# Gate logits turned by VectorE from four copies of the gate's columns, with routed loads and orders of VectorE rearranged

## What is computed

```
xn = layernorm(x)
x  = x + attn0(xn) + ffn0(xn)          # chunked linear attention; 16 experts of 128, all applied, weighted by sigmoids
xn = layernorm(x)
x  = x + attn1(xn) + ffn1(xn)

attn1: gate_logits = xn @ gate_W                    # (T, 4); top 2, softmax -> comb
       g, v, d = xn @ Wg[m] + bg[m], ...            # m = 0..3
       h_t = a_t * h_(t-1) + sigmoid(g)*tanh(v),  a = 0.001 + 0.998*sigmoid(d)
       out = sum over m of comb[:, m] * h[m]
ffn1:  gate_logits = xn @ gate_w.T + gate_b + expert_bias   # (T, 8)
       e = argmax(gate_logits)                      # one expert per token
       out = relu(xn @ w1[e] + b1[e]) @ w2[e] + b2[e]       # 256 -> 1024 -> 256
```

## Time and profile before

| | |
|---|---|
| median of 3 timed runs | 1025.59 us (1025.57, 1025.59, 1028.11) |
| profiled execution, its own time | 1028.48 us |
| span of its profile | 1026.8 us |
| TensorE busy | 1016.7 us, 99% |
| VectorE, ScalarE, GpSimd busy | 793.2 us (77%), 626.2 us (61%), 373.9 us (36%) |
| HBM read and written | 109.20 MB, 42.27 MB |

### The profile page before, as it was taken

The page is one execution under the profiler, slowest core; times in us unless marked ns, Lnnn a source line. Parts: engine busy times, 40 slices in busy tenths (PEclk is TensorE's granted clock), DMA queues, the critical chain, the costliest instruction groups (busy, mean ns, idle before and its releaser), DMA issues.

```text
span 1026.8 us, 20067 instructions
## 1 busy us (share of the span) xinstructions
PE 1016.7 (99%) x6432; PEld 908.7 (88%) x6432; DVE 793.2 (77%) x1307; ACT 626.2 (61%) x1179; POOL 373.9 (36%) x376
## 2 busy tenths in 40 slices
PE   8999999999999999999999999999999999999998
PEld 7988989989898988989877888999999999888887
DVE  6876767667685777969789998977788778588887
ACT  4554445535444454555566667888889888566665
POOL 3443443444444453443552775122122110482000
PEclk9999999999999999999999999999999999999999
DMA  6226313122132221442546376688897885652203
GB/s 190 69 83 221 103 41 82 55 79 70 41 82 82 81 82 62 144 165 63 194 157 245 116 286 221 199 249 250 267 286 249 284 262 182 230 178 68 92 11 102
DMA packets 112130, 152.12 MB, mean 148 GB/s; under 512 B 40720, under 2 KB 80656, under 8 KB 111056
## 3 DMA queue, kind: packets, MB, share of 16 engines
q1 hardware_dynamic: 100368, 132.35, 39.3%
q0 software_dynamic: 6016, 13.51, 4.5%
q10 hardware_dynamic: 5696, 5.64, 1.7%
HBM read 109.20 MB, written 42.27 MB: 148 GB/s over the span
## 4 chain that ended last, share of the span: by engine, by line
PE 86%; DVE 4%; DMA 3%; issue 3%; SPq 2%; ACT 2%; DVEq 0%; POOL 0%; ACTq 0%; POOLq 0%
PE ps L395 17%; PE ps L393 17%; PE ps L394 17%; PE ps L1194 6%; PE ps L1195 6%; PE ps L1196 6%; DMA raw<-w 2%; PE ps L1597 2%; PE ps L1598 2%; PE ps L1599 2%; PE ps L1212 2%; PE ps L1213 2%; PE ps L1214 2%; PE ps L1263 1%; PE ps L1256 1%
## 5 line engine op out<-in xcount | busy, mean ns | idle before, releaser
L827 POOL TENSOR_TENSOR acc<-acc,ytmp 128x512 f32<-128x512 f32 x120 | 157.7, 1314 | 243.3 <-ACT ytmp L918 223.4
L1637 ACT ACTIVATE act_o<-ps,scan_bias 128x512 f32<-128x512 f32 x189 | 129.5, 688 | 98.1 <-PE ps L395 94.1
L918 ACT ACTIVATE ytmp<-ps,sel 128x256 f32<-128x256 f32 x256 | 107.3, 471 | 95.7 <-PE ps L1196 95.1
L995 DVE SCALAR_TENSOR_TENSOR hT_l<-ps,hT_h 128x512 fp32r<-128x512 f32 (+1 forms) x136 | 88.4, 655 | 87.7 <-ACT hT_h L878 87.6
L1194 PE MATMUL ps<-vals_h,hT_h 128*128 128x256 f32 x512 | 144.9, 283 | 0.1
L1195 PE MATMUL ps<-vals_l,hT_h 128*128 128x256 f32 x512 | 143.8, 281 | 0.0
L1196 PE MATMUL ps<-vals_h,hT_l 128*128 128x256 f32 x512 | 143.5, 280 | 0.0
L878 ACT ACTIVATE hT_h<-ps 128x512 fp32r<-128x512 f32 x128 | 76.3, 596 | 89.4 <-PE ps L395 84.9
L1811 POOL DMA_DIRECT2D rows<-xs_d x92 | 52.8, 575 | 175.2 <-DVE sT L2045 163.8
L1980 DVE TENSOR_TENSOR_SCAN h_b<-a_b,hstate,xs_b 128x512 f32<-128x512 f32 x63 | 88.1, 1398 | 28.2 <-ACT a_b L1644 24.8
L1040 DVE SCALAR_TENSOR_TENSOR acc<-ps,sel,acc 128x256 f32<-128x256 f32 x240 | 104.0, 475 | 3.0 <-PE ps L1196 2.9
(11 more groups left out here) (261 smaller groups left out, 2769.6 us busy)
## 6 DMA issues: line engine op xcount, KB each, us to landing
raw<-w SPq DMA_DIRECT2D x78, 512.0 KB, 5.4
x1T<-xT_d SPq DMA_DIRECT2D x16, 512.0 KB, 5.5
comb_b<-comb_d SPq DMA_DIRECT2D x8, 1024.0 KB, 8.5
xn_d<-xn SPq DMA_DIRECT2D x15, 512.0 KB, 2.9
w_small<-w SPq DMA_DIRECT2D x14, 512.0 KB, 5.1
xs_d<-zeros ACTq DMA_DIRECT2D x1, 4992.0 KB, 19.5
x_d<-x SPq DMA_DIRECT2D x8, 512.0 KB, 4.5
xT_d<-nT_h SPq DMA_DIRECT2D x8, 512.0 KB, 2.7
```

Of the source, the lines that this page charges most:

```text
L827: pool.tensor_tensor(dst[:, 2:4, :], acc[:, 2:4, :], ytmp[:, k % 2, :, :], ALU.add).then_inc(acc23, 1)
L918: act.activation(ytmp[:, k % 2, j - 2, :], yb(k, j), ACT.Copy, scale=sel[:, j, k:k + 1]).then_inc(y_23, 1)
L1637: act.activation(act_o[:, i % 2, w, :], ps[:, 3 * (i % 2) + w, :], func, bias=scan_bias[:, w, i:i + 1]).then_inc(act_g, 1)
```

## The change

The gate's weight tile `gw` gets four copies of 32 columns (12 high, 12 low, 8 of zeros), so that its product has the same 32 rows on each quarter of the partitions. ScalarE copies, of each quarter, the tokens that belong there: four copies of 32 x 128 for one of 24 x 512. VectorE transposes the 32 x 32 blocks of the result in one instruction of 128 x 128 and sums high and low parts from SBUF. `post_rows` and its four transposes on TensorE are gone, with their use of bank 6, so the bank is freed by ScalarE's last copy.

In the routed stage VectorE's `rows_out` of a small slot moves behind the first `low_e` of the next slot, and in a small slot `w2_half(n, 1)` moves behind the first `low_e`. On SP the load of b2 of a small slot is issued ahead of w2's second half, and `w1_small` is loaded in slot 1 of a round, behind b1, for slot 0. The ranking moves from slots 21 and 22 to slots 1 and 2 of round 0.

```diff
@@ -89,8 +89,6 @@
     ebias = keep("ebias", [P, E1], F32)
     gate_b = keep("gate_b", [P, E1], F32)
     logits = keep("logits", [P, TILES, NL], F32)
-    gw = keep("gw", [P, DC, 2, NL], F32R)
-    gw_raw = keep("gw_raw", [P, DC, NL], F32)
     hstate = keep("hstate", [P, MC], F32)
     neg_half = keep("neg_half", [P, JT], F32)
     pos_i = keep("pos_i", [P, TILES], I32)
@@ -156,7 +154,10 @@
     stats1 = ra("stats1", [P, JT, 6], F32)
     mv1 = ra("mv1", [P, JT, 2], F32)
     rstd1 = ra("rstd1", [P, JT], F32)
-    lgT = ra("lgT", [P, GT], F32)
+    lgT = ra("lgT", [P, JT, Q32], F32)
+    lg_rows = ra("lg_rows", [P, JT, Q32], F32)
+    gw = ra("gw", [P, DC, P // Q32, Q32], F32R)
+    gw_raw = ra("gw_raw", [P, DC, Q32], F32)
     nq = x1[:].rearrange("p j (h k) -> p (j h) k", k=DC * Q32)
     end_a = ra.at
 
@@ -362,24 +364,24 @@
     O_STEP = 11
 
 
-    USES = ["v01", "v23", "q", "g", "s", "o", "op", "lg", "lt"]
-    POST = ("t1", "lg", "lt")
+    USES = ["v01", "v23", "q", "g", "s", "o", "op", "lg"]
+    POST = ("t1", "lg")
 
     def use(g, name, first=False):
 
-        start = 2 if first else 9 * g
+        start = 2 if first else 8 * g + 1
         return start + USES.index(name)
 
     def freed(g, name, first=False):
 
-        start = 2 if first else 8 * g
+        start = 2 if first else 7 * g + 1
         return start + [u for u in USES if u != "op"].index(name) + 1
 
     def post_use(g, name):
 
         if isinstance(g, int) and g == GROUPS - 1:
             n = POST.index(name)
-            return 9 * GROUPS + n, 2, 8 * GROUPS + n + 1
+            return 8 * GROUPS + 1 + n, 2, 7 * GROUPS + n + 2
         return use(g + 1, name), None, freed(g + 1, name)
 
     def wait_alone(eng, s, value):
@@ -408,10 +410,15 @@
         act.wait_ge(side_full, n + 1)
         act.activation(dst, src, ACT.Copy).then_inc(side_hi, 1)
 
-    def logits_T(act, n):
-
-        act.wait_ge(side_full, n + 1)
-        act.activation(lgT[0:2 * NL, :], ps[0:2 * NL, 6, :], ACT.Copy).then_inc(side_free, 1)
+    def logits_T(act, g):
+
+
+        act.wait_ge(side_full, post_use(g, "lg")[0] + 1)
+        act.wait_ge(lg_turned, g + 1)
+        for q in range(P // Q32):
+            quarter = slice(q * Q32, (q + 1) * Q32)
+            tokens = ps[quarter, 6, :].rearrange("p (j t) -> p j t", j=JT)[:, :, quarter]
+            act.activation(lgT[quarter], tokens, ACT.Copy).then_inc(side_free if q == P // Q32 - 1 else lg_T, 1)
 
     def ln_stats(dve, x, st, bn, tiles=range(JT)):
         for j in tiles:
@@ -445,9 +452,12 @@
         ln_norm(dve, xn1, x1, mv1, rstd1, rs1, xn1s, g, tiles)
 
     def gate_logits(dve, g):
-        dve.wait_ge(side_full, post_use(g, "lt")[0] + 1)
-        parts = ps[:, 6, 0:JT * 2 * NL].rearrange("p (j h n) -> p j n h", j=JT, h=2)
-        dve.tensor_reduce(logits[:, bass.ds(g * JT, JT), :], parts, AX.X, ALU.add).then_inc(side_free, 1)
+        dve.wait_ge(lg_T, (P // Q32 - 1) * (g + 1))
+        dve.wait_ge(side_free, post_use(g, "lg")[2])
+        dve.transpose(lg_rows[:].rearrange("p j n -> p (j n)"), lgT[:].rearrange("p j t -> p (j t)")).then_inc(lg_turned, 1)
+        dve.wait_ge(lg_turned, g + 2)
+        parts = lg_rows[:, :, 0:2 * NL].rearrange("p j (h n) -> p j n h", h=2)
+        dve.tensor_reduce(logits[:, bass.ds(g * JT, JT), :], parts, AX.X, ALU.add).then_inc(lg_ok, 1)
 
     def turned_part(c):
 
@@ -479,17 +489,9 @@
         else:
             pe.wait_ge(nT_ok, DC * (g + 1))
         for c in range(DC):
-            gate = gw[:, c].rearrange("p h n -> p (h n)")
-            pe.matmul(ps[0:2 * NL, 6, :], gate, nT_h[:, c, :], start=c == 0, stop=False)
-            last_mm = pe.matmul(ps[0:2 * NL, 6, :], gate, nT_l[:, c, :], start=False, stop=c == DC - 1)
-        last_mm.then_inc(side_full, 1)
-
-    def post_rows(pe, g):
-
-        wait_alone(pe, side_free, post_use(g, "lg")[2])
-        for j in range(JT):
-            last_mm = pe.transpose(ps[:, 6, 2 * j * NL:2 * (j + 1) * NL], lgT[0:2 * NL, j * P:(j + 1) * P],
-                                   ident[0:2 * NL, 0:2 * NL])
+            gate = gw[:, c].rearrange("p q n -> p (q n)")
+            pe.matmul(ps[:, 6, :], gate, nT_h[:, c, :], start=c == 0, stop=False)
+            last_mm = pe.matmul(ps[:, 6, :], gate, nT_l[:, c, :], start=False, stop=c == DC - 1)
         last_mm.then_inc(side_full, 1)
 
     def mixture_rank(dve, link, mx, j):
@@ -919,7 +922,7 @@
                                        scale=sel[:, j, k:k + 1]).then_inc(y_23, 1)
                     if k == 3 and first:
                         act.wait_ge(small_in, 16 * 4)
-                        act.activation(gw[:, :, 0, :], gw_raw[:], ACT.Copy).then_inc(gw_ready, 1)
+                        act.activation(gw[:], gw_raw[:].unsqueeze(2).to_broadcast((P, DC, P // Q32, Q32)), ACT.Copy).then_inc(gw_ready, 1)
                     if k == 2:
                         act.wait_ge(side_full, use(g, "g", first) + 1)
                         act.activation(sig_g[:], side2, ACT.Sigmoid).then_inc(side_free, 1)
@@ -1102,7 +1105,8 @@
                         decay_mask()
                     if k == 5 and first:
                         dve.wait_ge(gw_ready, 1)
-                        dve.tensor_tensor(gw[:, :, 1, :], gw_raw[:], gw[:, :, 0, :].bitcast(F32), ALU.subtract).then_inc(gw_ready, 1)
+                        gate = gw_raw[:, :, 0:NL].unsqueeze(2).to_broadcast((P, DC, P // Q32, NL))
+                        dve.tensor_tensor(gw[:, :, :, NL:2 * NL], gate, gw[:, :, :, 0:NL].bitcast(F32), ALU.subtract).then_inc(gw_ready, 1)
                         dve.tensor_tensor(ebias[:], ebias[:], gate_b[:], ALU.add).then_inc(e_bias, 1)
                     if k == 5 and last:
                         dve.wait_ge(acc_ip, GROUPS)
@@ -1277,8 +1281,6 @@
                             post_logits(pe, g - 1)
                     if k == E0 - 3 and last:
                         mixture_transpose(pe, mix1, 1, 7).then_inc(mix_full, 1)
-                    if k == E0 - 2 and not first:
-                        post_rows(pe, g - 1)
 
 
             pe.wait_ge(consts, 7)
@@ -1431,13 +1433,16 @@
                     ahead.clear()
                 if not zero(n):
                     store_y(*((r, k - 1) if k else (r - 1, ROUND - 1)))
+                if small(k):
+                    load_b2(expert_at(r, k))
                 if left(r, k) > 0:
                     raw2_half(n + 1, 1, expert_at(r, k + 1))
-                load_b2(expert_at(r, k))
-                if left(r, k) > 1 and k == 0 and not zero(r):
-                    load_w1_small(r, expert_at(r, ST))
+                if not small(k):
+                    load_b2(expert_at(r, k))
                 if left(r, k) > 1:
                     load_b1(n + 2, k + 2, expert_at(r, k + 2))
+                if left(r, k) > 0 and k == 1 and not zero(r):
+                    load_w1_small(r, expert_at(r, ST))
                 if not small(k) and bigs_left(r, k) > 1:
                     e = expert_at(r, k + ROUND)
                     raw1_half(bigs(r, k) + ST, 0, e)
@@ -2082,27 +2085,31 @@
                 low_e(0, 3, SLOT)
                 w1_half(1, 0)
 
+            RANKS2 = [(1, 3), (2, 1), (2, 2), (2, 3)]
+
             def low_halves(r, k):
 
                 n, (_, st) = ROUND * r + k, blocks(r, k)
                 for q in range(FJ // 2):
                     low_e(n, q, st * P)
-                    if left(r, k) == 1:
-                        mixture_rank(dve, link, mix2, q)
+                    if zero(r) and (k, q) in RANKS2:
+                        mixture_rank(dve, link, mix2, RANKS2.index((k, q)))
                     if q == 2 and not small(k):
                         for ahead in range(k + 1, next_big(k) + 1):
                             if left(r, k) > 0:
                                 turn_rows(r, ahead)
                     if q == 0 and k == 0:
+                        rows_out(r - 1, ROUND - 1)
+                    if q == 0 and k != 1:
                         w2_half(n, 1)
                     if q == (2 if k == 0 else 1) and not small(k) and bigs_left(r, k) > 0:
                         w1_half(bigs(r, k) + 1, 0)
 
             def slot(r, k):
                 n, (_, st) = ROUND * r + k, blocks(r, k)
-                if not zero(n):
-                    rows_out(*((r, k - 1) if k else (r - 1, ROUND - 1)))
                 if not zero(n) and k > 0:
+                    rows_out(r, k - 1)
+                if k == 1:
                     w2_half(n, 1)
                 if zero(n):
                     first_halves()
@@ -2114,8 +2121,9 @@
                     if not small(k) and bigs_left(r, k) > 0:
                         w1_half(bigs(r, k) + 1, 1)
                     w2_half(n + 1, 0)
+                if zero(r) and small(k):
+                    mixture_top(dve, link, mix2)
                 if left(r, k) == 0:
-                    mixture_top(dve, link, mix2)
                     mixture_finish(dve, link, mix2, 2)
 
             g = GROUPS - 1
```

(2 more changed lines are left out.)

16 lines of the change are left out of this document (8 added, 8 removed).

## The result

| | before | after |
|---|---|---|
| median of the timed runs | 1025.58 us (4 runs, 1024.40 to 1028.11) | 1033.8 us (4 runs, 1030.35 to 1038.87) |
| profiled execution | 1028.48 us, span 1026.8 | 1030.35 us, span 1028.7 |
| first start in the routed stage (first matmul of slot 0) | 645.4 us | 645.5 us |
| length of the routed stage (first to last start of a matmul) | 235.9 us | 238.2 us |

The ratio is 1.007, with an interval from 1.0047 to 1.0093: slower by 0.7%, where 0.6% faster was forecast. Two of the four runs of the changed kernel took 1030.4 us at a granted clock of 1.0, two about 1038 at 0.996 to 0.998, and the profile is of one of the shorter.

A forecast was written before the change was run, and what follows sets the result against it. TensorE, busy 1016.7 of 1026.8 us, was taken as the bound. Gate part -3.8 and routed stage -2.4 summed to -6.2 us, taken off the median of 1025.59: 1019.4 us, range 1015.5 to 1023.5.

The forecast's parts named there:

- the second at 0.15: Rival for the gate groups: copies at 0.25 us pitch, gate part only -1.8, total -4.2, 1021.4 us; chance 0.15.
- Transposes gone, 0.56 a group: Gate logits on TensorE: removing the row transposes saves 0.56 us in each of eight groups, 4.5 us at most.
- Four copies from 130.58 let hT_h start at 131.25 or at 131.58: ScalarE before the last `down`: hT_h started at 131.18; 131.25 taken, giving -3.8 us, or -1.8 at the slow bound.
- The estimate of 1.6 us for the four: ScalarE's four copies by the skill's budget: `down` 1 us late in seven groups, total about 1026; 0.04 of the 0.15.
- VectorE turns the logits, hidden: End of a gate body: VectorE's transpose adds some 0.3 us per group, hidden in 1.06 us of idle time.
- Small slots -1.8: Routed stage, five small slots: the first low part comes in time, closing TensorE's gap before the second layer, -1.8 us.
- slot 21 -0.75: Round 7's slot that held the ranking and a 0.76 us wait falls to its neighbours' level, -0.75 us.
- w1 wait of round 1 -1.45: At 693.86 ScalarE's wait for a half of w1, queued behind w1_small, goes: -1.65 less 0.2 given back.
- Round 0's small slot +1.0: This slot also carries the ranking, ten small operations between low parts; late by about 1.5 us against 0.5, +1.0.
- w1_small "+0.4 in all": Later load of w1_small: 5.4 us of room against 5.1 us from issue to landing, so +0.4 us in all.
- the rival: w1_small late every round: beyond 5.4 us latency TensorE idles at six small slots; 1031.6 us at 7.5; chance 0.10.
- First big slots "+0.5 ... b2's load is in front": First big slots: w2's second-half loads come about 0.4 us later, +0.5 us over seven slots.

The follow-up runs named there:

- e8: Kernel before plus the gate part, with ScalarE's four copies placed behind hT_h and xT_h, routed stage as before: 1023.15 us, ratio 0.9963.
- e1: Kernel before plus the change's gate part alone, routed stage as before: 1026.33 us, ratio 0.9995.
- e5: Changed kernel with all four ScalarE copies reading and writing partitions 0 to 31, so other experts are chosen: 1038.17 us in one run, not read as a result.
- e13: e12 with VectorE's small-slot order as in the change: 1044.17 us, kernel before 1043.03 on the same chip; stage 233.6 us.
- e14: Same kernel as e13 on another chip: 1049.14 us, kernel before 1053.43 there; stage 234.5 us.
- e7: Kernel before with only the w1_small load moved from slot 0 to slot 1, behind b1: 1033.46 us, ratio 1.0070.
- e15: e8 with b2 loaded ahead of w2's second half in small slots: 1054.92 us, kernel before 1053.43 on the same chip; stage 239.9 us.
- e16: Same kernel as e8, on the chip of e14 and e15: 1046.60 us, kernel before 1053.43 there; stage 232.7 us.
- e2: Changed kernel with w1_small loaded in the first slot of a round again, ahead of b1: 1033.01 us, ratio 1.0051.
- e4: Changed kernel with w1_small's load back in the first slot and ScalarE's copies behind hT_h and xT_h: 1028.51 us, ratio 1.0014.
- e9: e4 with VectorE's small-slot order back, w2's second half converted ahead of the first low part: 1029.44 us, ratio 1.0017.
- e11: e9 with b2's load back behind w2's second half in small slots: 1023.37 us, ratio 0.9957.
- e12: e11 with the four ranking pieces all in round 0's second big slot: 1022.82 us, ratio 0.9952.
- e10: e4 with w2's second half converted behind the third pair of tiles, not the first, in first big slots: 1036.28 us, ratio 1.0090.
- e3: Changed kernel with ScalarE's four copies moved behind hT_h and xT_h: 1033.47 us, ratio 1.0078.

## Why the prediction was wrong

The forecast was 6.2 us faster, the medians say 8.2 slower. Two terms failed. The greater is w1_small: +0.4 became +7.8. The other is the pitch of ScalarE's copies: -3.8 became 0. The first was named among the rivals, at 0.10, the second at 0.15 with too small a price; that b2's place costs was not foreseen at all.

- *Transposes gone, 0.56 a group:* right. e8 saves it; what it didn't count is the x1T wait of 1.1 us that follows.
- *"Four copies from 130.58 let hT_h start at 131.25 or at 131.58", pitch 0.17 or 0.25:* the first step that failed. The pitch was 0.29, outside both bounds, since I took it from neighbours that work on the same 128 partitions; each copy works on other 32 than the one before. hT_h started at 131.64 and the -3.8 us became 0 (e1). The Trainium skill, "VectorE: DVE Perf Modes", section "Two Vector instructions with no wait between them", says of VectorE that an instruction whose operand starts in another group of 32 partitions than that of the last instruction on the same memory starts only when every earlier one has finished. e5 shows the same for ScalarE here, 0.29 against 0.16 us. The estimate of 1.6 us for the four that the prediction drew from the Trainium skill, "ScalarE: Activation LUTs", section "Rules for kernel authors", was about as far above the 1.15 from first copy to hT_h as my 0.67 was below it.
- *VectorE turns the logits, hidden:* right. Transpose and sum took 0.30 and 0.25 us and nobody waited for them in the body.
- *Small slots -1.8, slot 21 -0.75, w1 wait of round 1 -1.45:* read off the two profiles they are -2.2 (six slots, 41.5 us before and 39.3 after), -0.9 and -1.7. But e13 and e14 show the first as worth nothing net that could be told. The third is luck as far as the runs show: in e1 the wait is gone too, with the load where it was.
- *Round 0's small slot +1.0:* +0.45 (6.98 to 7.43) between these two profiles. In e1, e7, e8, e15 and e16, none with the ranking there, the slot takes 6.5 us, so against those it is +0.9. Eight small operations stand between its low parts, not ten.
- *w1_small "+0.4 in all":* the step that failed by most, +7.8. "5.1 us from issue to landing now" was the median of first and second halves together; the second halves, which decide, took 5.8 to 6.8 in five of six rounds before, against 5.4 of room. The argument against the rival, that the megabyte moved was itself what made the queue long, failed too: in its new place the second half took 5.9 to 6.7 us. The rival's line (nothing up to 5.4 us, beyond it idle time in six slots) held; its chance was what I got wrong. e7 has this loss alone.
- *First big slots "+0.5 ... b2's load is in front":* in the changed kernel nothing, and that is luck: the loss showed only when the small load went back (e2, e4). By itself b2's place costs 5 to 7 us (e9 and e11, e15 and e16). I priced its issue, 0.4 us, not the transfer ahead of a load that has 2 to 4 us of room.

By profiled executions: gate 0, routed stage +2.3 us (7.8 of w_small, less the gains of the slots). The other 6 us of the difference in medians lie in where each profiled execution stands among its own runs, and are only in part explained (the clock, above).

## What to carry to other kernels

A load that is moved is priced by the room that is left (landing to use), against the longest latency that this very piece shows in the same stretch of the round, not a median over pieces that differ; and every small load put ahead of one with little room counts with its transfer. Where an in-order engine converts a load between evictions, the load's lateness is paid by all that stands behind it, and moving the conversion back delays the next load into the same buffer and all that is queued behind that load. After undoing one loss, look again: the first may have been covering a second, here of 5 to 8 us each. And a gain read off one pair of profiles is worth a second pair: the 1.39 us of the earlier trace rows went without the change that was to remove it. The version worth keeping is e8 or e12: the gate part with the copies behind hT_h and xT_h, and none of the load moves.

## What the runs showed of the hardware that I had not expected

- Four ScalarE copies, each on another group of 32 partitions than the one before, do not overlap: 0.29 us of pitch for 0.27 of duration, against 0.16 for 0.25 when all four start at partition 0. hT_h behind them, from partition 0 again, is held too (it starts 0.02 us after the last copy's end; in e5 it overlaps by 0.09).
- One load of one size has very different latencies: the second half of w2, 512 KB, took 5.9 us in e11, 6.8 in e9 and 8.2 in e4's round 4. While that last one was under way, from 761.5 to 769.7 us, the DMA share was 0.84 at 270 GB/s.
- The granted clock fell to 0.50 for a stretch of 3.4 us behind waits of TensorE of 2.1 to 3.3 us in e5, e7 and e10, and stayed at 1.00 behind one of 3.2 us in e3 and one of 2.1 us in e10 (693 us). In e13 TensorE idled 2.2 and 2.7 us (599 and 606 us), and the clock was 0.50 from 610.2 to 613.6; in the changed kernel's profile it is 1.00 throughout that stretch. What TensorE waited for there, on those two chips only, was not followed up.
